# One 256 KB write per copy pair of the sent experts, first-half reads ahead of the second's, two more banks for the last products

## The chip, the cores and the metric

The kernel runs on one core of a Trainium2 chip, in one launch. The metric is the device time in microseconds (us). The host only lays arrays out, and that is not timed. TensorE (PE) multiplies and transposes, VectorE (DVE), ScalarE (ACT) and GpSimd (POOL) work on elements, and SyncE (SP) issues nearly all DMAs. All data is float32 at the interface.

## The reference

A gated block on 16 batches of 128 tokens with 256 channels: x gains tanh(g) times a causal cross attention (16 heads), and then tanh(g) times a mixture of experts on the layer norm of the result. The expert part decides this case:

```python
grouped = x.reshape(B, g, t, d)                     # 64 groups of t = 32 tokens
logits = jnp.einsum('bgtd,des->bgtes', grouped, controller) + tie
perm = (logits == jnp.max(logits, axis=-3, keepdims=True))   # one token for each expert e and set s
dispatched = jnp.einsum('bgtd,bgtes->bgesd', grouped, perm)
inner = relu(jnp.einsum('bgesd,desf->bgesf', dispatched, f1) + bias)     # 32 experts, 4 sets, 32 wide
intermediate = jnp.einsum('bgesf,esfd->bgesd', inner, f2)
out = jnp.einsum('bgesd,bgtes->bgtd', intermediate, perm)
```

Every group of 32 tokens has 128 slots (32 experts x 4 sets), and each slot picks one token. There are 64 groups, so the experts' results are 64 x 128 rows of 256 floats, 8 MB.

## The kernel before

The attention runs up to about 160 us. The routing (logits, choice, gathering the chosen tokens into `routed`) runs to about 200 us, and there SP also loads the weights of the 32 experts into `wx`, 256.5 KB each. What follows is the part that the change touches.

**Expert stage.** The experts are taken in 16 pairs p. For pair p+1 PE computes the inner products (`expert_in`, L856), ACT and DVE apply bias and relu (`hidden`, L1133 and L1441), and for pair p PE computes the outputs (`expert_out`, L874 or L883) into two PSUM banks, of which ACT copies one and DVE the other (`keep_y`, L1143 or L1146, and L1451 or L1454). In the last step a product sums over the 128 slots of one group, so it needs the slots on partitions. The two kinds of pairs come to that in different ways:

- **Kept pairs** (8 of them, real experts 16 to 31) give a transposed output that is copied back into `routed`. At the end PE transposes it (`transpose_y`, L915, 16 blocks) and ACT (three blocks of four) or DVE (every fourth) copies it to partitions 0 to 63 of `y0` or `yw` (L1161, L1468).
- **Sent pairs** (`SENT`, real experts 0 to 15) go through DRAM. Both copies of a pair, one for each t, hold on 128 partitions (c, g) = 2 x 64 the rows of two experts. `send_rows` (L401) writes each copy as two DMAs of 64 partitions and 128 KB, so a pair has four DMAs. `y_rows` is a DRAM tensor [64 slots][64 groups][256 floats]. `load_rows` (L412) reads it back with slots on partitions 64 to 127, in 4 quarters (two sent pairs each) by 2 halves of the groups: `late` = 0 fills `y0` (blocks 0 to 7), `late` = 1 fills `yw`, which lies over expert weights and so also waits for the first 8 pairs. Each of the 8 reads has 512 KB.

There are YR = 4 buffers for sent copies. SP executes its program in order: a wait in it holds back all that follows. Its order is sends 0, 1, 2, load (0, early), sends 3, 4, load (1, early), sends 5, 6, load (2, early), send 7, load (0, late), load (3, early), loads (1 to 3, late), and then the 16 stores of the result (L433).

**Last stage.** PE runs transposes 0 to 3 and then, for each block b, transpose b+4 and `combine(b)` (L930): eight small matmuls of the one-hot `permT` with `y0` or `yw`. Combine 0 waits for the four early loads, combine 8 for the four late ones. Its result goes to bank b % 2. DVE adds it times the gate to `xs` (L1477), SP stores it. Transposes use banks 2 to 7 in turn. With two banks, combine b waits until DVE has done b - 2:

```python
if b >= 2:
    pe.wait_ge(yo_ready, b - 1)
```

The order of slots inside `routed` and `permT` follows from how POOL rearranges the routing weights (L556, four small copies) and from `EXPERTS`, the order in which experts are placed.

Of the kernel before, what the change touches and what calls it, by code (L numbers as in the profile page):

```python
# [21 lines left out]
ALU = mybir.AluOpType  # L22
# [4 lines left out]
NB = 16  # L27
E = 256
# [9 lines left out]
T = 32  # L38
# [18 lines left out]
PAIRS = NE // 2  # L57
HALF = P // 2
BIAS_SETS = 4
SENT = (0, 1, 3, 4, 6, 7, 9, 10)  # L60
KEPT = tuple(p for p in range(PAIRS) if p not in SENT)
EXPERTS = tuple(e for p in range(PAIRS) for e in
                ((SENT.index(p) // 2 + 4 * (SENT.index(p) % 2), SENT.index(p) // 2 + 4 * (SENT.index(p) % 2) + 8) if p in SENT
                 else (PAIRS + 2 * KEPT.index(p), PAIRS + 2 * KEPT.index(p) + 1)))
YR = 4
OVER = 4 * KH * E * 2 + (1 + 2 * 3) * KH * P - 4 * P
G2 = GROUPS // 2
# [8 lines left out]
def build(nc, x, ctxT, wattn, gbo, ctrl, wexp, constf, out):  # L76
    with ExitStack() as ctx, ExitStack() as early, ExitStack() as routing:
# [23 lines left out]
        tg = sb("tg", [P, 2])  # L101
# [71 lines left out]
        def columns(e, c):  # L173
            return bank[e % HR][:, 0:2 * GROUPS].rearrange("p (k c x) -> p c k x", c=2, k=2)[:, c]

        y_rows = nc.dram_tensor("y_rows", (HALF, GROUPS, E), F32).ap()
        sent = [[ring[:, i, t, :] for t in range(2)] for i in range(2)] + [[xn[:, 2 * t:2 * t + 2, :].rearrange("p a x -> p (a x)") for t in range(2)],
                [u[:, :, :, :].rearrange("p a h x -> p (a h x)") for u in (rp, ctrl2)]]

# [103 lines left out]
        def _(sp):  # L283
# [106 lines left out]
            def send_rows(q):  # L390

                p = SENT[q]
                first = EXPERTS[2 * p]
                for t in range(2):
                    if t == 0:
                        sp.wait_ge(y_kept_act, p + 1)
                    else:
                        sp.wait_ge(y_kept_dve, p + 1)
                    for c in range(2):
                        at = (2 * c + t) * 16 + first  # L400
                        sp.dma_start(y_rows[at:at + 9:8].rearrange("e g j -> g e j"),  # L401
                                     sent[q % YR][t][c * HALF:(c + 1) * HALF].rearrange("g (e j) -> g e j", e=2))\
                            .then_inc(y_sent[q % YR], 16)

            def load_rows(quarter, late):

                for q in (2 * quarter, 2 * quarter + 1):
                    sp.wait_ge(y_sent[q % YR], 4 * 16 * (q // YR + 1))
                if late:

                    sp.wait_ge(e_done, PAIRS // 2)
                sp.dma_start((y0, yw)[late][HALF + quarter::4, :].rearrange("s (k x) -> s k x", k=2),  # L412
                             y_rows[quarter::4].rearrange("s (k l x) j -> s k l (x j)", k=2, l=2)[:, :, late])\
                    .then_inc(y_loaded[late], 16)

            send_rows(0)
            send_rows(1)
            send_rows(2)
            load_rows(0, 0)
            send_rows(3)  # L420
            send_rows(4)
            load_rows(1, 0)
            send_rows(5)
            send_rows(6)
            load_rows(2, 0)
            send_rows(7)
            load_rows(0, 1)
            load_rows(3, 0)
            for quarter in range(1, 4):
                load_rows(quarter, 1)  # L430
            for b in range(NB):
                sp.wait_ge(yo_ready, b + 1)
# [5 lines left out]
        def _(pool):  # L438
# [90 lines left out]
            for n in range(SLOTS_N):  # L529
                s, g = n % 8, n // 8  # L530
                if n == 3 or s % 4 == 0 and 1 <= n // 4 - 1 < NB:
                    split_max(n // 4 - 1 if n > 3 else 0)
                if 0 <= n - LT < CH:
                    drop_above(n - LT)
                if s % 4 == 0 and 0 <= n // 4 - 4 < NB:
                    split_out(n // 4 - 4)
                if n == 3 or s == 1 and 2 <= g + 1 < NG2:
                    low_part(qp, 2, qr, 1, g + 1, qm_ready, ql_ready)
                if s == 3 and g + 2 < NG2:
                    low_part(kp, 0, kr, 1, g + 2, km_ready, kl_ready)  # L540
                if n == 16:
                    weight_low(WO)
                if s % 4 == 2 and n // 4 < NB:
                    if n == 2:
                        pool.wait_ge(bo_ready, 1)
                    bias_x(n // 4)
                if n == CH - 8:
                    pool.wait_ge(consts_loaded, 16)
                    pool.tensor_tensor(parity[:, :], groupmask[:, 0:2], groupmask[:, 2:4], ALU.add).then_inc(parity_step, 1)
                    pool.wait_ge(parity_step, 1)  # L550
                    pool.tensor_scalar(shut[:, :], parity[:, :], -1.0, -SHUT, ALU.add, ALU.mult).then_inc(parity_step, 1)
                    pool.wait_ge(small_loaded, 16)
                    for k in range(2):
                        for c in range(2):
                            at = (1 - k) * HALF + c * 32
                            last = pool.tensor_copy(  # L556
                                ctrl_sb[:, :, at:at + 32].rearrange("p h (t e) -> p h t e", t=2),
                                ctrl_in[:, :, k * HALF:(k + 1) * HALF].rearrange("p h (e t c) -> p c h t e", t=2, c=2)[:, c])
                    last.then_inc(ctrl_ready, 1)
                if s == 5 and g + 3 < NG2:  # L560
                    context_low(g + 3)
                if CH <= n < CH + 3:
                    split_rows(n - CH, n - CH)
# [22 lines left out]
        def _(pe):  # L586
# [254 lines left out]
                route(b)  # L841


            def expert_in(e):

                kind, at = int(EXPERTS[e] < PAIRS), EXPERTS[e] % PAIRS
                pe.wait_ge(wx_loaded[e], 16)
                if e >= HR:

                    if e % 2 == 0:  # L850
                        pe.wait_ge(h_ready_act, (e - HR) // 2 + 1)
                    else:
                        pe.wait_ge(h_ready_dve, (e - HR) // 2 + 1)
                for h in range(KH):
                    for t in range(2):
                        last = pe.matmul(bank[e % HR][t * HALF:(t + 1) * HALF, 0:2 * GROUPS],  # L856
                                         wx[:, e, h * P + t * HALF:h * P + (t + 1) * HALF],
                                         routed[:, h, kind].rearrange("p k s x -> p (k s) x")[:, at + 16 * t::32, :],
                                         start=(h == 0), stop=(h == KH - 1),
                                         tile_position=(0, t * HALF), skip_group_check=True)  # L860
                last.then_inc(h_done, 1)
# [36 lines left out]
                expert_out(p)  # L898


            BC = bank[0:2]

            def kept(b):

# [14 lines left out]
            def combine(b):  # L919
                late = b // (NB // 2)  # L920
                kept(b)
                if b % (NB // 2) == 0:

                    pe.wait_ge(y_loaded[late], 4 * 16)
                if b >= 2:
                    pe.wait_ge(yo_ready, b - 1)
                for g in range(NG):
                    k, i = g // 2, g % 2
                    at = k * YK + (b % (NB // 2) * 2 + i) * E
                    last = pe.matmul(BC[b % 2][g * T:(g + 1) * T, 0:E],  # L930
                                     permT[:, b, g * T:(g + 1) * T],
                                     (y0, yw)[late][:, at:at + E], start=True, stop=True, tile_position=(0, g * T))
                last.then_inc(c_done, 1)
# [12 lines left out]
        def _(act):  # L946
# [189 lines left out]
            def keep_y(p):  # L1136
                act.wait_ge(e_done, p + 1)
                if p in SENT:
                    q = SENT.index(p)
                    if q >= YR:  # L1140

                        act.wait_ge(y_sent[q % YR], 4 * 16 * (q // YR))
                    act.activation(sent[q % YR][0], bank[4 + 2 * (p % 2)], ACT.Copy).then_inc(y_kept_act, 1)  # L1143
                else:
                    at = KEPT.index(p) * 2 * G2
                    act.activation(by_set[:, 0, :, :, at:at + 2 * G2],  # L1146
                                   bank[4 + 2 * (p % 2)].rearrange("p (h c x) -> p h c x", h=KH, c=4), ACT.Copy)\
                        .then_inc(y_kept_act, 1)
# [18 lines left out]
        def _(dve):  # L1167
# [276 lines left out]
            def keep_y(p):  # L1444
                dve.wait_ge(e_done, p + 1)
                if p in SENT:
                    q = SENT.index(p)
                    if q >= YR:

                        dve.wait_ge(y_sent[q % YR], 4 * 16 * (q // YR))  # L1450
                    dve.tensor_copy(sent[q % YR][1], bank[5 + 2 * (p % 2)]).then_inc(y_kept_dve, 1)  # L1451
                else:
                    at = KEPT.index(p) * 2 * G2
# [19 lines left out]
            for b in range(NB):  # L1473
                if b % 4 == 1 and b + 4 < NB:
                    keep_ys(b + 4)
                dve.wait_ge(c_done, b + 1)
                dve.scalar_tensor_tensor(xs[:, b, :], bank[b % 2][:, 0:E], tg[:, 1:2], xs[:, b, :], ALU.mult, ALU.add)\  # L1477
                    .then_inc(yo_ready, 1)


# [51 lines left out]
```

## Time and profile before

| | |
|---|---|
| median of 3 runs | 263.15 us (263.0 to 264.95) |
| the profiled execution | 263.96 us |
| its span, first to last instruction | 262.2 us |
| mean granted TensorE clock | 0.979 of full speed |
| PE busy | 219.7 us, 84% |
| DVE busy | 202.1 us, 77% |
| ACT busy | 166.3 us, 63% |
| POOL busy | 128.9 us, 49% |

Times in the trace count from the start of the span; 1.76 us of the profiled execution lie outside it. A busy share is a mean over stages that have different limits. So what counts is, in each stage, which wait ends last. DMA-issuing instructions are not counted as busy, but they take time on SP, and the trace shows each one with its start and duration. "Landing" of a DMA counts from the start of its issue.

### The profile page before, as it was taken

The page shows a single profiled execution, that of the slowest core. Times are in us where ns is not written, and L with a number is a line of the kernel's source. Part 1 is how long each engine was busy: PE and PEld are TensorE (multiplying, and loading weights), DVE is VectorE, ACT ScalarE, POOL GpSimd, SP SyncE. Part 2 cuts the span into 40 slices and gives each one's busy share as a digit, 9 for nine tenths or more (in the row PEclk, how much of TensorE's full clock was granted, in tenths as well). Part 3 has the DMA queues.
Part 4 walks back from the last instruction along what each step waited for, and adds up shares of the span by engine and source line. Part 5 has one row for each costly group of instructions (what it writes and reads, how often), then busy time and mean ns, then how long its engine had stood idle before and what let it go on. Part 6 is the DMA issues. An engine that isn't in the chain of part 4 may idle for free.

```text
span 262.2 us, 7559 instructions
## 1 busy us (share of the span) xinstructions
PE 219.7 (84%) x2849; PEld 171.3 (65%) x2850; DVE 202.1 (77%) x472; ACT 166.3 (63%) x356; POOL 128.9 (49%) x243
## 2 busy tenths in 40 slices
PE   0474687798987999999899999969998999985992
PEld 0464576576765788787677777747776777872550
DVE  4896847789999699696899899999995555553563
ACT  2633766768667868596678775338786555546570
POOL 5652165658746767886487969446572000000000
PEclk9997979999999999999999999999999999998899
DMA  7747689931434344325220000018994587999723
GB/s 213 213 100 201 166 222 227 232 108 50 135 106 135 85 134 110 90 61 143 65 61 6 6 4 6 2 35 314 388 384 168 120 187 211 245 241 202 186 99 124
DMA packets 32231, 37.92 MB, mean 145 GB/s; under 512 B 4099, under 2 KB 27331, under 8 KB 31939
## 3 DMA queue, kind: packets, MB, share of 16 engines
q1 hardware_dynamic: 31661, 36.82, 50.9%
q10 hardware_dynamic: 534, 0.61, 0.8%
q8 instruction: 23, 0.38, 0.7%
q14 instruction: 13, 0.11, 0.1%
HBM read 18.26 MB, written 6.29 MB: 94 GB/s over the span
## 4 chain that ended last, share of the span: by engine, by line
PE 30%; DVE 19%; POOL 17%; issue 12%; DMA 11%; ACT 7%; SPq 3%; ACTq 0%; POOLq 0%; DVEq 0%
POOL pT L481 6%; DVE rsum L1275 4%; PE banks L731 4%; PE banks L753 4%; PE banks L930 3%; DMA y_rows<-ctrl 3%; PE banks L915 3%; PE banks L856 3%; DVE nmax L1267 3%; PE banks L602 3%; DMA y<-y_rows 2%; SPq L401 2%; DMA xs<-in_x_dram 2%; PE banks L711 2%; ACT pT L1022 2%
## 5 line engine op out<-in xcount | busy, mean ns | idle before, releaser
L481 POOL TENSOR_SCALAR_AFFINE_SELECT pT<-pT 128x512 f32<-128x512 f32 x64 | 40.8, 640 | 34.6 <-ACT pT L1022 34.3
L1267 DVE TENSOR_REDUCE nmax<-banks 128x4 f32<-128x512 f32 x64 | 43.7, 682 | 14.8 <-PE banks L665 14.7
L1027 ACT ACTIVATE banks<-cb 128x512 f32<-128x512 bf16 x62 | 37.0, 597 | 12.8 <-DVE nmax L1267 11.1
L1022 ACT ACTIVATE pT<-banks 128x512 f32<-128x512 f32 x64 | 37.5, 586 | 3.0 <-PE banks L682 2.9
L711 PE MATMUL banks<-pT,va 128*32 128x128 f32 x512 | 27.3, 285 | 0.9 <-POOL pT L481 0.8
L1275 DVE RECIPROCAL rsum<-banks 128x256 f32<-128x256 f32 x16 | 27.9, 1746 | 0.0
L665 PE MATMUL banks<-kst,qst 96*128 96x128 bf16 x256 | 25.4, 222 | 2.1 <-ACT banks L1027 2.1
L682 PE MATMUL banks<-qst,kst 99*128 99x128 bf16 x256 | 25.4, 221 | 1.2 <-DMA qst<-nT 1.0
L711 PE MATMUL banks<-pT,ones 128*32 128x128 f32 x512 | 25.7, 273 | 0.0
L1115 ACT ACTIVATE routed<-banks 128x512 f32<-128x512 f32 x30 | 17.2, 626 | 5.6 <-PE banks L753 5.6
L594 PE MATMUL banks<-cf,xn 128*128 128x128 f32 x32 | 6.0, 317 | 17.2 <-DVE xn L1220 14.2
L1042 ACT ACTIVATE onh<-on 128x256 fp32r<-128x256 f32 x16 | 6.7, 417 | 20.1 <-DVE on L1281 19.9
L665 PEld LDWEIGHTS banks<-kst,qst 96*128 96x128 bf16 x256 | 17.0, 99 | 3.5 <-ACT banks L1027 2.9
L682 PEld LDWEIGHTS banks<-qst,kst 99*128 99x128 bf16 x256 | 15.2, 98 | 5.3 <-issue 1.3
L856 PE MATMUL banks<-routed,wx 128*64 128x128 f32 x256 | 17.3, 278 | 0.8 <-ACT routed L1115 0.8
L1220 DVE TENSOR_SCALAR xn<-xs,mv,rs 128x256 f32<-128x256 f32 x32 | 16.8, 531 | 0.1
L856 PEld LDWEIGHTS banks<-routed,wx 128*64 128x64 f32 x256 | 13.7, 136 | 4.4 <-issue 2.7
L594 PEld LDWEIGHTS banks<-cf,xn 128*128 128x128 f32 x32 | 4.1, 159 | 17.9 <-issue 9.0
L711 PEld LDWEIGHTS banks<-pT,ones 128*32 128x32 f32 x512 | 15.3, 110 | 0.0
L711 PEld LDWEIGHTS banks<-pT,va 128*32 128x32 f32 x512 | 10.1, 108 | 7.9 <-POOL pT L481 1.3
L1477 DVE SCALAR_TENSOR_TENSOR xs<-banks,tg,xs 128x256 f32<-128x256 f32 x16 | 7.5, 483 | 9.4 <-PE banks L930 9.3
L505 POOL TENSOR_TENSOR onl<-on,onh 128x256 fp32r<-128x256 f32 x16 | 11.7, 732 | 2.9 <-ACT onh L1042 2.9
(133 smaller groups left out, 624.4 us busy)
## 6 DMA issues: line engine op xcount, KB each, us to landing
wx<-in_wexp_dram SPq DMA_DIRECT2D x32, 256.5 KB, 8.1
kst<-kp SPq DMA_DIRECT2D x48, 128.0 KB, 2.6
qst<-qp SPq DMA_DIRECT2D x48, 128.0 KB, 2.4
cT<-in_ctxT_dram SPq DMA_DIRECT2D x8, 256.0 KB, 3.3
y_rows<-ring SPq DMA_DIRECT2D x16, 128.0 KB, 3.4
y<-y_rows SPq DMA_DIRECT2D x4, 512.0 KB, 5.3
wx<-y_rows SPq DMA_DIRECT2D x4, 512.0 KB, 8.8
out_dram<-xs SPq DMA_DIRECT2D x16, 128.0 KB, 1.9
```

The costliest lines, as they stand in the source:

```text
L481: pool.affine_select(p, p, [[0, HC], [1, P]], ALU.is_ge, 0.0, base=0, channel_multiplier=-1)\
L505: pool.tensor_tensor(onl[:, b % 2], on[:, b % 2], onh[:, b % 2].bitcast(F32), ALU.subtract)\
L665: last = pe.matmul(to[:, j * P:(j + 1) * P], qst[0:SROWS, g % STACKS, h, b % 2, :], kst[0:SROWS, g % STACKS, h, b % 2, :], start=False, st ...
L682: last = pe.matmul(to[:, j * P:(j + 1) * P], kst[0:TROWS, g % STACKS, h, b % 2, :], qst[0:TROWS, g % STACKS, h, b % 2, :], start=True, sto ...
L711: last = pe.matmul(BO[b % 2][j * DP:(j + 1) * DP, at + o * P:at + (o + 1) * P], left, pT[:, n % PR, j * P:(j + 1) * P], start=(e == 0 and ...
L856: last = pe.matmul(bank[e % HR][t * HALF:(t + 1) * HALF, 0:2 * GROUPS], wx[:, e, h * P + t * HALF:h * P + (t + 1) * HALF], routed[:, h, ki ...
L1022: act.activation(pT[:, n % PR, :], BT[n % 2], ACT.Exp, scale=float(D) ** -0.5).then_inc(p_ready, 1)
L1027: act.activation(BS[n % 2], causal, ACT.Copy).then_inc(mask_placed, 1)
L1115: last = act.activation(by_group(t, b), by_column(bank[((3, 6), (4, 5))[b % 2][t]]), ACT.Copy)
L1220: dve.tensor_scalar(xn[:, b % 4, :], xs[:, b, :], mv[:, b, 0:1], rs[:, b:b + 1], ALU.subtract, ALU.mult).then_inc(ready, 1)
L1267: dve.tensor_reduce(nmax[:, b % 2, :].rearrange("p (e j o) -> p e o j", e=2, o=KH)[:, e, o], BS[n % 2].rearrange("p (j t) -> p j t", j=HC) ...
L1275: dve.reciprocal(rsum[:, :, :], BO[b % 2][:, E:2 * E].rearrange("p (h t) -> p h t", h=KH))\
```

## The change

- `SENT` becomes pairs 0, 1, 2, 4, 5, 6, 8, 9, where it was 0, 1, 3, 4, 6, 7, 9, 10. The number of sent pairs stays 8.
- The slots are laid out in another order, so that a whole copy (128 partitions, two experts) is one DMA of 256 KB. Sent pair q fills rows 8q to 8q + 7 of `y_rows`, and a quarter is 16 rows that lie together.
- SP's order becomes sends 0 to 4, early load 0, send 5, early load 1, send 6, early load 2, send 7, early load 3, and then late loads 0 to 3.
- The routing weights are rearranged by three POOL copies, one of 64 columns per half and two of 32.
- `expert_in` reads the sent experts' columns of `routed` through a pattern with one more level.
- Combines 12 and 13 go to banks 6 and 7, which the transposes no longer need by then. Combines 12 and 13 wait for no earlier DVE result, 14 and 15 for the one four blocks (10, 11) back.

```diff
-SENT = (0, 1, 3, 4, 6, 7, 9, 10)
+SENT = (0, 1, 2, 4, 5, 6, 8, 9)
+        by_copy_rows = y_rows.rearrange("(i t c) g j -> t (c g) i j", t=2, c=2)
...
-                    for c in range(2):
-                        at = (2 * c + t) * 16 + first
-                        sp.dma_start(y_rows[at:at + 9:8].rearrange("e g j -> g e j"),
-                                     sent[q % YR][t][c * HALF:(c + 1) * HALF].rearrange("g (e j) -> g e j", e=2))\
-                            .then_inc(y_sent[q % YR], 16)
+                    sp.dma_start(by_copy_rows[t, :, first:first + 2, :],
+                                 sent[q % YR][t].rearrange("p (e j) -> p e j", e=2)).then_inc(y_sent[q % YR], 16)
...
-                             y_rows[quarter::4].rearrange("s (k l x) j -> s k l (x j)", k=2, l=2)[:, :, late])\
+                             y_rows[rows].rearrange("s (k l x) j -> s k l (x j)", k=2, l=2)[:, :, late])\
...
-            send_rows(0)
-            send_rows(1)
-            send_rows(2)
+            for q in range(5):
+                send_rows(q)
             load_rows(0, 0)
-            send_rows(3)
-            send_rows(4)
+            send_rows(5)
             load_rows(1, 0)
-            send_rows(5)
             send_rows(6)
             load_rows(2, 0)
             send_rows(7)
-            load_rows(0, 1)
             load_rows(3, 0)
-            for quarter in range(1, 4):
+            for quarter in range(4):
                 load_rows(quarter, 1)
...
-                    for k in range(2):
-                        for c in range(2):
-                            at = (1 - k) * HALF + c * 32
-                            last = pool.tensor_copy(
-                                ctrl_sb[:, :, at:at + 32].rearrange("p h (t e) -> p h t e", t=2),
-                                ctrl_in[:, :, k * HALF:(k + 1) * HALF].rearrange("p h (e t c) -> p c h t e", t=2, c=2)[:, c])
+                    pool.tensor_copy(ctrl_sb[:, :, HALF:].rearrange("p h (j q) -> p h q j", q=4),
+                                     ctrl_in[:, :, 0:HALF].rearrange("p h (q j) -> p h q j", q=4))
+                    for c in range(2):
+                        last = pool.tensor_copy(
+                            ctrl_sb[:, :, c * 32:(c + 1) * 32].rearrange("p h (t e) -> p h t e", t=2),
+                            ctrl_in[:, :, HALF:].rearrange("p h (e t c) -> p c h t e", t=2, c=2)[:, c])
...
+            def sent_at(e, t):
+                return ((e % 4) * 4 + 2 * t) * 4 + e // 4
...
-                                         routed[:, h, kind].rearrange("p k s x -> p (k s) x")[:, at + 16 * t::32, :],
+                                         routed[:, h, 1, :, sent_at(at, t):sent_at(at, t) + 5:4, :] if kind else
+                                         routed[:, h, 0].rearrange("p k s x -> p (k s) x")[:, at + 16 * t::32, :],
...
-            BC = bank[0:2]
+            BC = [bank[b % 2 if not 12 <= b < 14 else b - 6] for b in range(NB)]
...
-                if b >= 2:
+                if 2 <= b < 12:
                     pe.wait_ge(yo_ready, b - 1)
+                elif b >= 14:
+                    pe.wait_ge(yo_ready, b - 3)
```

## Rows read from the trace of the kernel before

**Rows 1.** Waits from 200 to 262.2 us: who waited for whom, total us, times, longest.
```profile
PE banks L930 <- DMA y<-y_rows: 3.0, 1, 3.0
PE banks L930 <- DVE xs L1477: 0.5, 2, 0.3
```

**Rows 2.** Chain that ended last, from 228 us: start us, us, what.
```profile
231.22 2.65 DMA y_rows<-ctrl
...
233.94 5.96 DMA y<-y_rows
...
240.04 0.64 PE banks L930 x8
...
245.20 0.57 PE banks L930 x8
...
254.90 0.61 PE banks L930 x8
```

**Rows 3.** Windows: us, busy us (count) of PE, PEld, DVE, ACT, POOL, clock, DMA share, GB/s.
```profile
200.00:234.00 34.00, 33.36 (x448) 26.88 (x448) 18.47 (x49) 17.62 (x49) 0.68 (x2) 1.00 0.71 180
237.00:240.00 3.00, 0.00 (x0) 0.00 (x0) 0.07 (x1) 2.92 (x6) 0.00 (x0) 1.00 1.06 213
241.00:244.00 3.00, 3.00 (x23) 1.25 (x22) 2.08 (x4) 0.40 (x1) 0.00 (x0) 0.50 0.96 197
245.00:254.00 9.00, 9.00 (x94) 4.92 (x93) 5.75 (x12) 6.20 (x11) 0.00 (x0) 1.00 0.43 136
...
218.50:219.00 0.50, 0.50 (x12) 0.33 (x8) 0.22 (x1) 0.50 (x3) 0.00 (x0) 1.00 1.18 395
```

**Rows 4.** Timeline of the expert stage: start us, us, engine, line, operation [idle before].
```profile
203.35 0.69 DVE L1451 COPY ring<-banks 128x512 f32<-128x512 f32 x1 [0.60 <-PE banks L874]
205.44 0.69 DVE L1451 COPY ring<-banks 128x512 f32<-128x512 f32 x1 [0.59 <-PE banks L874]
...
222.23 0.69 DVE L1451 COPY xn<-banks 128x512 f32<-128x512 f32 x1 [0.59 <-PE banks L874]
```

**Rows 5.** Timeline of SP: issue of each write (L401) and load (L412).
```profile
207.33 0.61 SPq L401 DMA_DIRECT2D y_rows<-ring  x1
207.98 1.90 SPq L401 DMA_DIRECT2D y_rows<-ring  x1
...
228.67 1.52 SPq L401 DMA_DIRECT2D y_rows<-rp  x1
```

**Rows 6.** Landings by source line: L401, the 32 writes; then L412, the 8 loads.
```profile
DMA to landing us min/median/max: 2.4/3.0/5.2
...
DMA to landing us min/median/max: 4.9/5.7/11.1
```

**Rows 7.** The same views of L287 (input loads) and L433 (stores): issue ns, min/median/max.
```profile
L287 SPq DMA_DIRECT2D xs<-in_x_dram x5: 442/471/707, 0.8 to 42.9; - x5
...
L433 SPq DMA_DIRECT2D out_dram<-xs x16: 332/333/417, 241.2 to 258.7; - x16
```

**Rows 8.** Timeline of the last stage's start.
```profile
234.51 2.49 PE L915 MATMUL banks<-cf,routed 128*128 128x128 f32 x20 [0.88 <-DVE routed L1454]
235.23 4.86 ACT L1161 ACTIVATE y<-banks 64x512 f32<-64x512 f32 x8 [0.96 <-PE banks L915]
235.68 1.39 DVE L1468 COPY y<-banks 64x512 f32<-64x512 f32 x2 [1.32 <-PE banks L915]
```

**Rows 9.** Timeline of the end.
```profile
255.54 0.92 DVE L1477 SCALAR_TENSOR_TENSOR xs<-banks,tg,xs 128x256 f32<-128x256 f32 x2 [0.73 <-PE banks L930]
...
258.20 0.48 DVE L1477 SCALAR_TENSOR_TENSOR xs<-banks,tg,xs 128x256 f32<-128x256 f32 x1 [0.41 <-PE banks L930]
```

**Rows 10.** Groups of POOL by form; L468 copies 128x128 with two inputs.
```profile
L468 POOL TENSOR_TENSOR wl<-w,wh 128x128 fp32r<-128x128 f32 x4 | 2.0, 536 | 3.2 <-ACT wh L970 3.2
L556 POOL COPY ctrl<-ctrl 128x64 f32<-128x64 f32 x4 | 1.0, 290 | 0.1
```

**Rows 11.** Groups by form from 200 us: PE reading `routed`.
```profile
L856 PE MATMUL banks<-routed,wx 128*64 128x128 f32 x256 | 17.3, 278 | 0.8 <-ACT routed L1115 0.8
```

More of the change, by code:

```diff
@@ L59 @@
 BIAS_SETS = 4
-SENT = (0, 1, 3, 4, 6, 7, 9, 10)
+SENT = (0, 1, 2, 4, 5, 6, 8, 9)
 KEPT = tuple(p for p in range(PAIRS) if p not in SENT)
-EXPERTS = tuple(e for p in range(PAIRS) for e in
-                ((SENT.index(p) // 2 + 4 * (SENT.index(p) % 2), SENT.index(p) // 2 + 4 * (SENT.index(p) % 2) + 8) if p in SENT
-                 else (PAIRS + 2 * KEPT.index(p), PAIRS + 2 * KEPT.index(p) + 1)))
+EXPERTS = tuple(2 * SENT.index(p) + i if p in SENT else PAIRS + 2 * KEPT.index(p) + i
+                for p in range(PAIRS) for i in range(2))
 YR = 4
@@ L398, in send_rows @@
                         sp.wait_ge(y_kept_dve, p + 1)
-                    for c in range(2):
-                        at = (2 * c + t) * 16 + first
-                        sp.dma_start(y_rows[at:at + 9:8].rearrange("e g j -> g e j"),
-                                     sent[q % YR][t][c * HALF:(c + 1) * HALF].rearrange("g (e j) -> g e j", e=2))\
-                            .then_inc(y_sent[q % YR], 16)
+                    sp.dma_start(by_copy_rows[t, :, first:first + 2, :],
+                                 sent[q % YR][t].rearrange("p (e j) -> p e j", e=2)).then_inc(y_sent[q % YR], 16)
             def load_rows(quarter, late):
                 for q in (2 * quarter, 2 * quarter + 1):
-                    sp.wait_ge(y_sent[q % YR], 4 * 16 * (q // YR + 1))
+                    sp.wait_ge(y_sent[q % YR], 2 * 16 * (q // YR + 1))
                 if late:
                     sp.wait_ge(e_done, PAIRS // 2)
+                rows = slice(quarter * 16, (quarter + 1) * 16)
                 sp.dma_start((y0, yw)[late][HALF + quarter::4, :].rearrange("s (k x) -> s k x", k=2),
-                             y_rows[quarter::4].rearrange("s (k l x) j -> s k l (x j)", k=2, l=2)[:, :, late])\
+                             y_rows[rows].rearrange("s (k l x) j -> s k l (x j)", k=2, l=2)[:, :, late])\
                     .then_inc(y_loaded[late], 16)
-            send_rows(0)
-            send_rows(1)
-            send_rows(2)
+            for q in range(5):
+                send_rows(q)
             load_rows(0, 0)
-            send_rows(3)
-            send_rows(4)
+            send_rows(5)
             load_rows(1, 0)
-            send_rows(5)
             send_rows(6)
@@ L929, in combine @@
                     at = k * YK + (b % (NB // 2) * 2 + i) * E
-                    last = pe.matmul(BC[b % 2][g * T:(g + 1) * T, 0:E],
+                    last = pe.matmul(BC[b][g * T:(g + 1) * T, 0:E],
                                      permT[:, b, g * T:(g + 1) * T],
@@ L1140, in keep_y @@
                     if q >= YR:
-                        act.wait_ge(y_sent[q % YR], 4 * 16 * (q // YR))
+                        act.wait_ge(y_sent[q % YR], 2 * 16 * (q // YR))
                     act.activation(sent[q % YR][0], bank[4 + 2 * (p % 2)], ACT.Copy).then_inc(y_kept_act, 1)
@@ L1448, in keep_y @@
                     if q >= YR:
-                        dve.wait_ge(y_sent[q % YR], 4 * 16 * (q // YR))
+                        dve.wait_ge(y_sent[q % YR], 2 * 16 * (q // YR))
                     dve.tensor_copy(sent[q % YR][1], bank[5 + 2 * (p % 2)]).then_inc(y_kept_dve, 1)
@@ L1476, in _ @@
                 dve.wait_ge(c_done, b + 1)
-                dve.scalar_tensor_tensor(xs[:, b, :], bank[b % 2][:, 0:E], tg[:, 1:2], xs[:, b, :], ALU.mult, ALU.add)\
+                dve.scalar_tensor_tensor(xs[:, b, :], bank[b % 2 if not 12 <= b < 14 else b - 6][:, 0:E], tg[:, 1:2], xs[:, b, :], ALU.mult, ALU.add)\
                     .then_inc(yo_ready, 1)
```

## The prediction, made before the changed kernel ran

> **What bounds the kernel now.** I read the waits of the last 60 us first, then the chain of waits, then SP's own timeline. The waits show one stall of PE that is large: combine 0 waits 3.0 us for a load from `y_rows` [rows 1]. The chain says which load that is, and when: the last write of a sent pair is issued at 231.22, lands, releases early load 3 at 233.94, and 5.96 us later that load is there and combine 0 runs at 240.04 [rows 2]. Two things make it late. The pair that it needs is the eleventh of sixteen, and SP falls behind. The copies of a sent pair come every 2.09 us where two such pairs follow one another (203.35, 205.44 in rows 4), but a pair has four writes that begin 0.65 us apart, 2.6 us, and now and then an issue takes 1.5 to 1.9 us instead of 0.61 [rows 5]. The copy of the last sent pair, pair 10, ends at about 225.0 (pair 9's ends at 222.92 [rows 4], plus a period of 2.09), and yet its last write is issued only at 231.22: SP is 6.2 us behind.
>
> The stall costs more than itself. With PE idle for 3.0 us the granted clock, which was 1.00 from 200 to 234, is 0.50 of 2.4 GHz (the lower level, 1.2 GHz) from 241 to 244 and back at 1.00 from 245 on [rows 3]. Three periods of transpose and combine take 245.20 - 240.04 = 5.16 us, where the eight that follow take (254.90 - 245.20) / 8 = 1.21 us each [rows 2].
>
> Behind that, PE sets the pace at 1.21 us a block to combine 11 (254.90), and in the tail the two banks do: combines wait for DVE [rows 1], and DVE's last five results come at 255.54 and up to 258.20 in pairs with gaps [rows 9].
>
> **The change part by part, on the profiled execution (span 262.2, time 263.96).**
>
> *Writes.* 32 DMAs of 128 KB become 16 of 256 KB with the same pieces of 1 KB, twice as many in each. The trace has no such issue. Lower bound: 0.33 us, a store of 128 rows [rows 7]; upper bound: twice the present write, 1.22 us [rows 5]. The input loads, of 256 or 512 rows of 1 KB, take 0.44 to 0.71 us [rows 7], so the count of rows hardly matters; the shape of the pattern seems to. The pattern stays, so I take 0.65 us with its gap. A pair then costs SP 1.3 us, less than PE's period of 2.09 us, and SP waits for copies rather than the other way round.
>
> *Pairs and order.* The last sent pair is pair 9, whose DVE copy ended at 222.92 in this trace [rows 4]. Nothing ahead of it changes in length, since kept and sent pairs cost PE the same. SP's program after: early load 2 is just ahead of send 7 and waits for the writes of sends 4 and 5. Pair 6's copies end at 222.92 - 3 x 2.09 = 216.6, its second write is issued by 217.3 and lands after 2.4 to 5.2 us [rows 6], by 222.5 at the latest. Load 2 then goes out at about 222.5, and send 7 at 222.9 and 223.6. That write lands after 2.4 to 5.2 us, so early load 3 is issued at 226.0 to 228.8. It lands after 4.9 to 5.96 us [rows 2, 6] (the 11.1 us in that row is of a late load, queued behind others): between 230.9 and 234.8.
>
> *Where PE is by then.* Transposes 0 to 4 end at 234.51 + 2.49 = 237.00 [rows 8], and that end does not depend on the loads. ACT's copy of block 0 ends at 235.23 + 4.86 / 4 = 236.45, and DVE's of block 1 at 237.07 [rows 8], ahead of the combines that need them. So combine 0 starts at 237.0, not 240.04: **3.04 us**. The margin over the load's latest landing is 2.2 us, and 6 us over its earliest. ACT needs 1.21 us for a block and has three of four, 0.91 us a block; DVE has 1.39 / 4 + 0.48 = 0.83. Both stay under PE's 1.21.
>
> *The clock.* With no idle stretch the first three periods should run at 1.21 us as the later ones do: 5.16 - 3 x 1.21 = **1.53 us**. Bounds: nothing, if the clock falls all the same, and 1.53. I take the whole, since the rows show 1.00 through 34 us of dense work before the stall [rows 3]. Combine 11 then starts at 237.0 + 11 x 1.21 = 250.3, 4.6 us before its 254.90.
>
> *Late loads.* Late load 0 no longer stands ahead of early load 3. All four go out between about 229 and 234. At the rate of the window in which only such loads ran, 213 GB/s from 237 to 240 [rows 3], 2 MB take 9.8 us, so they are there by some 245 us; combine 8 runs at 237.0 + 8 x 1.21 = 246.7. Hidden, though not by much: were they as late as before relative to their issue, PE would wait 1 us or so there.
>
> *Banks 6 and 7.* Before, DVE starts block 11 at 255.54 and block 15 at 258.20. A pair of DVE results takes 0.92 and one 0.48, so 0.44 us apart [rows 9]. Combines 12 to 15 now need DVE's results of 10 and 11 at the most, and PE needs 0.57 us for one at the most [rows 2]; in the pairs it already keeps up with DVE's 0.44. DVE would start block 15 at 255.54 + 4 x 0.44 = 257.30: **0.90 us**. Bounds: 0.4, if PE gives one per 0.57 us, and 0.9. The store behind it takes what it took.
>
> *POOL.* Four copies take 1.0 us together. One of 128x128 (no more than the 0.54 us of the two-input L468) and two of 128x64 (0.25 each) give 0.8 to 1.04 us [rows 10]: within 0.2 us either way, and I take nothing. *The columns of `routed`:* L856 already reads four runs of 32 floats at a stride; a further level changes no count of columns. I take nothing. The three slot orders cost no instruction.
>
> Sum: 3.04 + 1.53 + 0.90 = 5.5 us, so the profiled execution would take 263.96 - 5.5 = 258.5. The median of the runs is 0.8 under the profiled one, 263.15, and so the forecast is **257.7 us**. What is uncertain there: if the runs near 263.0 did not have the whole clock loss, the median gains less.
>
> A rule that speaks against the first step: the Trainium skill, "DMA: Bandwidth & Descriptors", section "Issuing engines are not separate DMA queues", says that the time a sequencer takes to start a DMA is usually small beside the transfer. The trace disagrees here: issues of 0.65 us for 128 KB make 200 GB/s, while loads and writes together reached 395 GB/s in a window [rows 3]. By the rule the writes would be bound by the DMA engines and the change would give only what the order and `SENT` give, which is the second rival below.
>
> **Rivals.**
>
> 1. *The clock falls all the same, or the runs never had the whole loss.* For it: 0.8 us between median and profiled run. Against: the clock falls only after the stall [rows 3]. Gain 3.04 + 0.90 = 3.9: 259.2 us. Chance 0.12.
> 2. *Issue or transfer stays the bound.* If a 256 KB issue costs 1.22 us, a pair costs SP 2.5 us as before; with two of the slow issues (+1.3 us each [rows 5]) SP ends send 7 at about 228.7, the write lands by 232, load 3 by 238.0. Combine 0 then starts at 238.0, the stall is 1 us, and the gain 2.0 + 0.9 + the clock's 0 to 1.5: 260.2 to 258.7 us. If instead the DMA engines move 1 KB pieces no faster than 200 to 230 GB/s, 4 MB of writes and three early loads end near 231, load 3 by 237: nearly nothing lost. Chance 0.10.
> 3. *The load is no earlier.* Something that the trace doesn't show (the writes' landing growing with their size, SP waiting at early load 2) holds load 3 until about 240. Only the tail is gained: 262.2 us. It takes a delay of over 5 us on the bounds above. Chance 0.05.
> 4. *Slower.* PE reads the four runs of a sent expert's columns with one more level and loses time on each of L856's 128 sent matmuls. At present one costs 17.3 / 256 = 0.068 us of PE's time [rows 11]. It decides from 5.5 / 128 = 0.043 us each; at twice that it would cost 8.7 us, net +3.2: 266.4 us. For it: no row has this pattern. Against: the same four runs at a stride cost nothing visible now [rows 11]. Chance 0.04.
>
> The forecast itself, 256.5 to 258.9 us, has 0.69.
>
> **How the numbers follow.** About 1% (2.6 us) is what a measurement of this kernel can tell from no change. The forecast, rival 1 and most of rival 2 are faster by over 1%: 0.69 + 0.12 + 0.07 = 0.88. The rest of rival 2 and rival 3 are within 1%: 0.08. Slower: 0.04. The range 256.5 to 260.3 takes in the forecast, rival 1 and most of rival 2, and leaves out misses of the sum by more than 1.2 us downward.
>
> **What would show it.** After: 16 write issues of about 0.61 us, SP waiting for copies; early load 3 issued at 226 to 229 and landed by 235; no wait of L930 on a DMA; 20 transposes at 234.5 and combine 0 right behind at 237; a granted clock of 1.00 from 237 to 246; a period of 1.21 us from the first block; the last five DVE results 0.44 us apart; L856 with an unchanged mean of 278 ns. The prediction is wrong if combine 0 or combine 8 still waits for a load, if the clock falls in that stretch, or if the expert stage's end moves from 234.4.

## The result

The changed kernel takes 260.04 us (median of 4 runs, 258.35 to 261.0), the kernel before beside it 264.05 us (263.0 to 266.31). The ratio is 0.9865, 95% interval 0.9818 to 0.9912. Two more measurements of the same two kernels (`after_again` and `after_third` below, on two chips) gave 0.9838 (0.9808 to 0.9868) and 0.9812 (0.976 to 0.9865). A ratio compares only runs within 1.5% of the fastest run of the same kernel, while a median is one of all runs. So the change is worth 1.6%, about 4.2 us, and the forecast was 2.1%, 5.5 us. The forecast time, 257.7, was 2.3 us too low: 0.9 of it because the kernel before takes 264 us and more in larger samples, not 263.15, and 1.5 because the gain was smaller.

The chain of waits of the changed kernel, from the first transpose of the last stage on (start us, us, what):

```profile
236.92 2.49 PE banks L914 x20
239.41 0.57 PE banks L931 x8
...
243.05 0.57 PE banks L931 x8
...
252.76 0.61 PE banks L931 x8
253.37 0.03 issue
253.39 2.21 DVE xs L1478 x5
```

It holds no DMA any more. Combine 0 follows the transposes at once (2.49 us after their start; before it was 5.53 [rows 2, 8]), three periods take 243.05 - 239.41 = 3.64 us (before 5.16), and DVE's last five results are one run of 2.21 us. The windows show that the granted clock stays at 1.00, the level of 2.4 GHz (columns as in rows 3):

```profile
240.00:241.00 1.00, 1.00 (x12) 0.59 (x12) 0.82 (x2) 0.96 (x3) 0.00 (x0) 1.00 0.81 164
243.00:244.00 1.00, 1.00 (x13) 0.59 (x12) 0.32 (x1) 0.96 (x3) 0.00 (x0) 1.00 1.30 262
```

SP's timeline (L399 writes, L410 loads) and, below it, its waits in that stretch:

```profile
216.86 0.36 SPq L399 DMA_DIRECT2D y_rows<-ring  x1
217.26 0.47 SPq L399 DMA_DIRECT2D y_rows<-ring  x1
...
225.15 0.52 SPq L410 DMA_DIRECT2D y<-y_rows  x1
225.71 1.69 SPq L399 DMA_DIRECT2D y_rows<-rp  x1
227.44 0.48 SPq L399 DMA_DIRECT2D y_rows<-ctrl  x1
232.12 0.52 SPq L410 DMA_DIRECT2D y<-y_rows  x1
232.75 0.53 SPq L410 DMA_DIRECT2D wx<-y_rows  x1
```

```profile
SPq L405 <- DMA y_rows<-ctrl: 4.1, 1, 4.1
SPq L405 <- DMA y_rows<-ring: 1.1, 1, 1.1
```

A 256 KB write is issued in 0.36 us and a second behind it in 0.47, less than a 128 KB one took before (0.61 [rows 5]). SP now waits for the copies. Early load 3 is issued 4.8 us ahead of the first transpose (before: 0.6) and lands 5.5 us later, 1.8 us before combine 0.

And yet the profiled execution is only 4.0 us shorter in its span, 258.2 against 262.2, although the stretch from the first transpose to the end went from 27.7 to 21.3 us. Of these 6.4 us, 3.04 are the stall, 1.52 the clock, 0.94 the banks, and 0.9 lie behind DVE's last result, where the last store took 3.5 us to the end of the span before and takes 2.6 now; no part of the change touches that store. On the other side, the first transpose itself comes 2.4 us later, at 236.92 instead of 234.51. The page's row of the granted clock, 40 slices of the span, shows where; first before, then after:

```profile
PEclk9997979999999999999999999999999999998899
```

```profile
PEclk9997779599999999999999999999999999999999
```

Before has its late fall (8 8, behind the stall), after has none; but in slices 5 to 8, 26 to 52 us, where both kernels run the same instructions, after has 7 7 9 5 where before has 9 7 9 9. The first row-sum reciprocal of DVE starts at 54.43 us before and at 56.98 after.

### The profile page after: what moved, and what is told of

It is laid out like the page before. It is cut to its first block, busy times and chain, and to the rows that moved or that the text cites. A ratio compares the mean times of both kernels' runs of the same rounds, so it can differ in the third digit from the quotient of the medians.

```text
span 258.2 us, 7540 instructions
## 1 busy us (share of the span) xinstructions
PE 221.8 (86%) x2849; PEld 174.9 (68%) x2850; DVE 204.4 (79%) x472; ACT 166.5 (64%) x356; POOL 128.9 (50%) x242
## 4 chain that ended last, share of the span: by engine, by line
PE 41%; DVE 20%; POOL 15%; issue 11%; ACT 6%; DMA 4%; ACTq 0%; SPq 0%; POOLq 0%; DVEq 0%
PE banks L854 6%; POOL pT L475 6%; DVE rsum L1276 4%; PE banks L914 4%; PE banks L725 4%; PE banks L747 4%; PE banks L596 3%; PE banks L882 3%; PE banks L873 3%; PE banks L705 3%; DVE nmax L1268 3%; PE banks L931 3%; DMA w<-in_wattn_dram 2%; PE banks L618 2%; DMA xs<-in_x_dram 2%
## 5 line engine op out<-in xcount | busy, mean ns | idle before, releaser
L659 PE MATMUL banks<-kst,qst 96*128 96x128 bf16 x256 | 26.1, 226 | 3.0 <-ACT banks L1028 2.8
L705 PE MATMUL banks<-pT,va 128*32 128x128 f32 x512 | 27.7, 289 | 0.7 <-POOL pT L475 0.7
L676 PE MATMUL banks<-qst,kst 99*128 99x128 bf16 x256 | 25.8, 224 | 0.3 <-ACT pT L1023 0.3
L659 PEld LDWEIGHTS banks<-kst,qst 96*128 96x128 bf16 x256 | 17.6, 101 | 4.4 <-ACT banks L1028 3.6
L596 PE MATMUL banks<-xTh,wh 128*128 128x256 f32 x32 | 11.8, 368 | 2.5 <-DVE xTl L1260 2.5
```

The source lines that it names most:

```text
L596: last = pe.matmul(to[:, o * E:(o + 1) * E], stationary, moving, start=(q == 0), stop=(q == len(parts) - 1))
L659: last = pe.matmul(to[:, j * P:(j + 1) * P], qst[0:SROWS, g % STACKS, h, b % 2, :], kst[0:SROWS, g % STACKS, h, b % 2, :], start=False, st ...
L676: last = pe.matmul(to[:, j * P:(j + 1) * P], kst[0:TROWS, g % STACKS, h, b % 2, :], qst[0:TROWS, g % STACKS, h, b % 2, :], start=True, sto ...
L705: last = pe.matmul(BO[b % 2][j * DP:(j + 1) * DP, at + o * P:at + (o + 1) * P], left, pT[:, n % PR, j * P:(j + 1) * P], start=(e == 0 and ...
```

## The experiments

All stages below are read from one profiled execution of each kernel, in us. "T0" is the start of the first transpose of the last stage. `before_look1` and `before_look2` are two more profiled executions of the kernel before.

| kernel | T0 | T0 to combine 0 | combine 0 to 3 | T0 to end |
|---|---|---|---|---|
| before | 234.5 | 5.53 | 5.16 | 27.7 |
| before_look1 | 235.7 | 5.32 | 3.70 | 24.6 |
| before_look2 | 237.6 | 4.71 | 5.08 | 25.9 |
| banks_only | 236.0 | 5.39 | 5.05 | 26.1 |
| filler | 236.8 | 6.61 | 3.70 | 25.9 |
| order_only | 237.8 | 3.71 | 3.79 | 24.7 |
| writes_only | 236.3 | 3.20 | 3.71 | 23.5 |
| old_pairs | 234.8 | 5.04 | 3.70 | 24.1 |
| late_load | 236.7 | 4.83 | 5.11 | 25.3 |
| by_expert | 236.0 | 2.48 | 3.63 | 21.2 |
| after | 236.9 | 2.49 | 3.64 | 21.3 |
| after_again | 237.9 | 2.48 | 3.64 | 21.7 |
| after_third | 238.9 | 2.49 | 3.64 | 21.6 |

**Is the later start the change's doing?** The changed and the unchanged kernel were run again.

> The changed kernel once more, timed in more rounds. Theory A: the stretch from the first transpose of the last stage to the end is fixed by the change (21.3 us, where before has 27.7) and what differs beside it lies in the first 54 us, where the code is the same and the granted clock falls by chance: then the mean gain over many rounds is 5 to 6.5 us, ratio 0.976 to 0.981, and another profile of the same kernel has another start (the first row-sum reciprocal anywhere from 53 to 58 us). Theory B: the changed kernel itself loses 2.5 us in its first part (another placement of code or data): then that reciprocal is at 57 us again and the ratio stays near 0.985.

> The kernel before once more, one look. Theory A (the profiled execution of before was an unusual one: early start of the last stage, full clock loss behind the stall): the first transpose comes later than 234.5 us, near the 236 to 238 us of five other profiled executions whose code is the same up to 145 us, and the stretch from there to the end is 26 to 27.7 us. Theory B (the changed kernel is slower in its first 54 us): the first transpose comes at 234.5 us again.

> The same kernel, a second look, to see how the stall (T0 to combine 0, 5.5 us), the three periods behind it (5.2 us with the clock at half, 3.6 without) and the last store (3.5 us or 2.6) vary. Theory A: the stall is the same within 0.3 us, the periods behind it are 5.0 to 5.2 in most looks. Rival 1 of the prediction: in some looks the clock stays at 1.00 and they take 3.7.

> The changed kernel beside the two above on the same chip: from the first transpose to combine 0 2.5 us, to the end 21.2 to 21.8 us, and the first row-sum reciprocal anywhere from 54.4 to 58 us. Runs near 260.2 us.

The ratio of after_again is 0.9838, outside the 0.976 to 0.981 of theory A and with an interval down to 0.9808; its row-sum reciprocal starts at 57.98 us. Both are nearer to what theory B expected. The three profiled executions of the kernel before have that reciprocal at 54.4 to 55.3 us and T0 at 234.5, 235.7 and 237.6, the three of the changed one have 57.0 to 58.0 and 236.9, 237.9 and 238.9. With the other kernels, whose first 145 us are the same code too, the difference shrinks: the six with the old slot layout average 55.4 us for the reciprocal and 236.4 for T0, the seven with the new one 56.5 and 236.8. The profiled execution on which the prediction was built has the earliest T0 of all thirteen. So these executions leave theory B open; the warmed kernels below decide it. From T0 on, the changed kernel repeats within 0.5 us and the kernel before varies by 3.1 us, in the stall (4.7 to 5.5), behind it, and in the landing of the last store. In before_look2 the clock fell again (1.01 and 1.05 us where 0.57 and 0.64 are the times at full clock):

```profile
242.28 0.64 PE banks L930 x8
242.91 0.64 PE banks L915 x4
243.56 1.01 PE banks L930 x8
244.57 1.05 PE banks L915 x4
```

In before_look1 it did not, with a stall of 2.8 us:

```profile
241.01 0.64 PE banks L930 x8
241.65 0.64 PE banks L915 x4
242.29 0.57 PE banks L930 x8
242.86 0.64 PE banks L915 x4
```

**One part at a time.** `order_only` is before with two edits, the new `SENT` and the new order of SP; `writes_only` is after with both old and two banks; `banks_only` is before with the edits of `BC` and its waits.

```diff
-SENT = (0, 1, 3, 4, 6, 7, 9, 10)
+SENT = (0, 1, 2, 4, 5, 6, 8, 9)
```

> The kernel before with only the new choice of sent pairs and the new order of SP; writes stay 128 KB (four a pair, 2.6 us of SP), banks stay two. Theory A (both SP's backlog and the late pair held the load back): pair 9's last write is issued at about 229 instead of 231.2 of the kernel before, early load 3 at 231.5 instead of 233.9, so combine 0 starts 2 to 3 us after where the kernel before has it relative to the transposes: stall 0.5 to 1.5 us, the clock's loss partly gone; gain 2 to 4 us from the first transpose on. Theory C (the order alone was enough): no stall, gain 4.6 us. Theory D (only the number of writes mattered): gain under 1 us.

> The changed kernel with the old choice of pairs, the old order of SP and two banks, so only the 256 KB writes with their slot layout. Pair 10's copy ends 9.4 us before the first transpose (225.1 of 234.5 in the kernel before). Theory A: writes are issued at once, land within 5 us, early load 3 is issued about 3.5 to 4 us before the first transpose and lands 1.5 to 2.5 us after it, before combine 0 is due at +2.5: no stall or under 0.5 us, the clock stays at 1.00, gain 4.6 us from the first transpose on. Theory C (order decides): late load 0, which stands ahead of early load 3, holds it back and a stall of over 1 us stays.

> The kernel before with banks 6 and 7 for combines 12 and 13. Theory A: the last five DVE results come 0.44 us apart, 0.9 us less from combine 11 on, the stall of 3.0 us and the clock at 0.50 behind it stay as they were. In the runs a gain of 0.3%, about what three rounds can't tell. Rival: the store queue or its landing takes it back, and the stretch from combine 11 to the end stays at 7.3 us.

Ratios: order_only 0.9898 (0.9858 to 0.9938), writes_only 0.987 (0.9826 to 0.9915), banks_only 0.9925 (0.9867 to 0.9983). Against the mean stall of 2.7 us in three executions of the kernel before, `order_only` has 1.2 and `writes_only` 0.7. With order and pairs alone SP issues its last write at 231.67, still late because pairs cost it 2.6 us, and combine 0 waits 1.2 us:

```profile
231.67 4.11 DMA y_rows<-ctrl
...
235.85 5.50 DMA y<-y_rows
241.35 0.14 issue
```

With the writes alone early load 3 goes out at 233.78 and lands 5.6 us later, and combine 0 runs 0.13 us behind that, 0.7 us after it could have:

```profile
233.78 0.52 SPq L410 DMA_DIRECT2D y<-y_rows  x1
239.50 0.64 PE L933 MATMUL banks<-y,permT 128*32 128x256 f32 x8 [0.71 <-ACT y L1164]
```

The profile puts these 0.71 us down to ACT, which copied until 239.45; but the copy that combine 0 needs is ACT's first, done by 237.6. Theory A had the load 1 to 1.5 us earlier and the stall under 0.5, theory C had over 1. The parts overlap: order and pairs alone take 1.5 of the mean 2.7 us, the writes alone 2.0, the rest needs both. banks_only shows DVE's five results in 2.21 us and the stall and the clock's fall as before; the tail is 0.94 us shorter, as expected (0.3%). By its ratio it gains 0.75%, with an interval that reaches to 0.2%; by the medians of all runs, 263.82 and 264.35 us, it gains 0.2%.

**The choice of pairs.** The changed kernel with only the old `SENT`:

> The changed kernel with the old choice of sent pairs (the last is pair 10, not 9), and with the new order, the 256 KB writes and the new banks. Theory A: the last send and early load 3 come one pair's time (2.1 us) later than in the changed kernel; early load 3 lands at about +2.5 to +3.2 us after the first transpose, so the choice of pairs is worth a stall of 0 to 0.7 us. Rival E (in the run with the writes alone it was late load 0, ahead in the queue, that held early load 3): no stall here, combine 0 at +2.5.

Both expectations fell. Combine 0 waits 2.5 us. The chain (start us, us, what) says why:

```profile
227.39 6.77 DMA y_rows<-ctrl
...
234.22 5.52 DMA y<-y_rows
```

The last write is issued 7.4 us ahead of T0 (9.5 in the changed kernel), as its pair comes 2.1 us later, and it lands after 6.8 us and not 4.6. Early load 2 stands right ahead of it (in the timeline of SP, old_pairs):

```profile
226.19 0.52 SPq L410 DMA_DIRECT2D y<-y_rows  x1
226.76 0.58 SPq L399 DMA_DIRECT2D y_rows<-rp  x1
227.39 0.47 SPq L399 DMA_DIRECT2D y_rows<-ctrl  x1
```

All 18 traces of this case say the same about that load. The last write lands 6.4 to 8.0 us after the issue of early load 2, whether it is issued 1.2 us behind it (and lands after 5.4 to 6.8 us) or 3.8 us behind it (2.7 to 2.9 us), and always after that load has landed. So the time of early load 3 follows from that of early load 2, and this one goes out 11.8 us ahead of T0 in the changed kernel, 8.7 in old_pairs and 7.1 in before. In the changed kernel and in old_pairs it waits for the second write of send 5, which belongs to pair 6 with the new `SENT` and to pair 7 with the old one. That the load's 512 KB hold the write is the reading of these traces; no run moved load 2 alone.

In this one profiled execution of old_pairs the choice of pairs is worth 2.5 us of stall, once the order is the new one. The order by itself is not shown to gain anything: old_pairs has writes_only's pairs and writes and the new order, and stalls for 2.5 us where writes_only stalls for 0.7. No run has the new pairs in the old order.

**Cut in two again.** The changed kernel with each copy in two DMAs by expert:

```diff
+                    for i in range(2):
+                        sp.dma_start(by_copy_rows[t, :, first + i, :],
+                                     sent[q % YR][t][:, i * E:(i + 1) * E]).then_inc(y_sent[q % YR], 16)
```

> The changed kernel with each 256 KB write cut in two again, by expert instead of by partition: 32 writes of 128 KB, each 128 partitions times 1 KB, the shape of the stores. Theory A (SP's time per pair and the place of the last sent pair decide, not the number of writes): an issue takes 0.33 us and 0.42 with its gap, a pair 1.7 us, under the 2.09 us period, so there is no stall and the kernel equals the changed one within 0.5 us. Rival (many small writes clog the transfers): early load 3 lands later and combine 0 waits.

From T0 on it is the changed kernel (2.48, 3.63, 21.2 us), with 32 writes as before. Its issues take 0.32 to 0.49 us, 128 rows of 1 KB over 128 partitions; the kernel before needed 0.61 for 128 rows of 1 KB over 64 partitions. So neither the number of writes nor that of rows mattered. The shape shortened both the issue and the landing of an undisturbed write (1.7 to 1.9 us, against 2.4 before), and this run does not part the two. Its ratio, 0.9898 with an interval of 0.9779 to 1.0018, says nothing beside that.

**The stall put back.** The changed kernel with `sp.wait_ge(e_done, PAIRS)` ahead of early load 3:

> The changed kernel with one wait more: SP issues early load 3 only after the last expert product, about 0.9 us before the first transpose, as the kernel before did by its backlog. All else of the change stays. Theory A: combine 0 starts 4.7 to 5.2 us after the first transpose instead of 2.5; the clock falls behind the stall or not, so the stretch from the first transpose to the end grows from 21.3 us by 2.2 to 2.7 us without the clock's fall and by up to 4.2 us with it; the runs lose 0.9 to 1.6% against the changed kernel. Rival: something else of the change (slot layout, columns of the experts) made the gain, and the stretch stays within 1 us of 21.3.

The ratio to the kernel before is 0.9952 (0.9923 to 0.9981), against 0.981 to 0.984 of the changed kernel: 1.1 to 1.4% come from this one load. The chain has it, with the clock's fall behind it:

```profile
235.84 5.54 DMA y<-y_rows
241.39 0.14 issue
241.52 0.64 PE banks L932 x8
242.16 0.64 PE banks L915 x4
242.81 0.89 PE banks L932 x8
243.69 1.05 PE banks L915 x4
244.74 1.01 PE banks L932 x8
```

**The clock behind the stall.** The kernel before with work for PE in the stall, output unused:

```diff
+                if b == 0:
+                    for _ in range(22):
+                        pe.transpose(bank[1][:, 0:P], ident, ident)
                 combine(b)
```

> The kernel before with 22 transposes of the identity into bank 1 between transposes 0 to 4 and combine 0. They fill 2.75 us of the 3.0 us in which PE waits for the load; their output is used by nothing. Theory A: combine 0 starts no earlier (5.5 us after the first transpose), the granted clock stays at 1.00, the next three periods take 3.64 instead of 5.16 us, and the runs gain up to 1.5 us (0.6%). Rival 1 of the prediction (the runs mostly don't have that loss): the profile shows the same, but the runs gain under 0.5 us.

The stall is there (6.6 us from T0, the load took 6.6 us in this execution), the three periods take 3.70 us. The ratio, 0.9969 (0.9912 to 1.0025), could not tell the rival.

**The start made steady.** PE waits at 18 to 24 us for the second pair of normalized blocks, 5.1 us in before, and comes out of it at the lower level: the granted clock is 0.50 from 23 to 25.8 us. Twenty transposes of the identity into bank 0 went there:

```diff
+            for _ in range(20):
+                pe.transpose(bank[0][:, 0:P], ident, ident)
             transpose_x(1, bank[3])
```

> The changed kernel with 20 transposes of the identity into bank 0, whose output is used by nothing, while PE waits for the second pair of normalized blocks at 18 to 24 us. Theory A (the different start of the runs comes from where the granted clock falls in the first 56 us): the clock stays at 1.00 from 20 to 28 us, where nine profiled executions had 0.59 to 0.79, the matmuls of that stretch end 1 to 1.5 us earlier after the wait, and the runs gain up to 1.5 us, unless the later falls (32 to 56 us) take it back. Rival F (the start is set by the loads and by DVE, the clock is only a sign): the first row-sum reciprocal stays between 54.4 and 58 us and the runs stay within 0.3%.

> The changed kernel with the 20 transposes ahead of the wait at 18 to 24 us, once more, beside the three above: near 257.9 us and 0.9755 of the kernel before.

Ratios 0.9755 (0.9723 to 0.9786) and 0.9788 (0.9731 to 0.9845), medians 257.93 and 258.73 us: about 2 us faster than the changed kernel, somewhat more than the up to 1.5 us of theory A. The granted clock is 1.00 from 20 to 28 us in warm. In the timeline of the kernel before and of warm, PE comes out of the wait like this (start us, us, what [idle before]):

```profile
22.99 1.12 PE L594 MATMUL banks<-cf,xn 128*128 128x128 f32 x4 [5.12 <-DVE xn L1220]
23.75 0.56 PE L602 MATMUL banks<-cTh,wh 128*128 128x256 f32 x1
```

```profile
20.12 2.35 PE L764 MATMUL banks<-cf 128*128 128x128 f32 x20
23.92 0.66 PE L588 MATMUL banks<-cf,xn 128*128 128x128 f32 x4 [1.46 <-DVE xn L1223]
24.33 0.37 PE L596 MATMUL banks<-cTh,wh 128*128 128x256 f32 x1
```

The same on the kernel before, without and with the filler in the stall, and once more with 20 transposes ahead of PE's first wait:

> The kernel before with the same 20 transposes of the identity, output unused, ahead of the wait at 18 to 24 us. Theory A (the start varies by chance and equally in both kernels): the first row-sum reciprocal comes at 54 to 55 us, the runs gain about 2 us (0.8%) on the kernel before, as the changed kernel did (0.9755 against 0.983), and stand 4.5 us above warm_again. Theory B (the changed kernel had lost something in its start that the filling gave back): no gain here, and warm_again is over 6 us faster.

> The same kernel and also 22 unused transposes into bank 1 in the stall ahead of combine 0. Theory A (the clock's fall behind the stall is in about two runs of three): 1.0 us (0.4%) faster in the runs than warm_before, the three periods behind the stall 3.7 us in the profile. Rival 1 of the prediction (the runs mostly don't have it): under 0.4 us. The full term of the prediction would be 1.5 us.

> The changed kernel with the 20 transposes of warm_again and 20 more as soon as the identity is loaded, at 4 to 9 us, when PE waits for the first normalized blocks; outputs unused. If PE's 256-column matmuls of 11 to 19 us take 0.41 us because the clock is low there, they take 0.28 us now and the start gains 1 to 2.5 us (0.4 to 1%) where PE sets the pace; if loads and DVE set it, under 0.5 us.

warm_before has 0.9903 (0.9858 to 0.9948), so the kernel before gains 1% by the same lines, and between it and warm_again lie 1.2% by the ratios, 3 us (4.4 us by the medians of all runs, 263.12 and 258.73), where theory B had over 6. T0 comes at 235.2 and 234.2 us in warm_before and warm_before_filler, and at 234.4 and 235.0 in warm and warm_again. The start of the changed kernel had lost nothing of its own: theory B falls. warm_before_filler has 0.9828 (0.9776 to 0.9881): 0.75% less than warm_before, 2 us, with intervals that overlap. That speaks for a clock term in the runs and against rival 1; filler without the warming gained 0.3%, so its size stays open. warm_both, 0.9756 (0.97 to 0.9813), is no different from warm_again. The transposes at 3.8 to 7.8 us do not bring the clock up for what follows, as this window of warm_both shows (columns as in rows 3, clock 0.50):

```profile
12.00:19.00 7.00, 5.92 (x28) 5.65 (x28) 7.00 (x13) 2.45 (x4) 3.81 (x4) 0.50 0.47 103
```

## Why the prediction was wrong, point by point

- **Direction and place: right.** The load from `y_rows` bound combine 0, and SP's backlog and the late pair made it late. Of the 6.4 us from T0 on in the profiled execution, 5.5 are where the steps put them.
- **The stall, 3.04 us: right in the profiled execution** (5.53 to 2.49 = 3.04), and too large for other executions: two more of the kernel before have 5.32 and 4.71, so it is 2.7 us on the mean of three.
- **The clock, 1.53 us: the step that failed, by its size.** I took the upper bound because the stretch before the stall had run at 1.00, as if every run lost it. Of seven profiled executions with a stall of over 2 us and no filler, five lost it (before, before_look2, banks_only, late_load, and warm_before with 5.16 us) and two did not (before_look1, old_pairs). Over the three executions of the kernel before the three periods take 5.16, 3.70 and 5.08, a mean 1.0 us over 3.64. In the runs the filler gave 0.8 us on the kernel before (0.9969) and about 2 us on the warmed one, each with 1.5 to 2 us of uncertainty, so the runs do not narrow that.
- **The banks, 0.90 us: right.** From combine 11 to the end of DVE's work it was 258.68 - 254.90 = 3.78 us, and is 2.84.
- **The last store, taken to be unchanged: luck in the profiled execution.** Behind DVE's last result the span goes on for 3.5 us before and 2.6 after, and this 0.9 us, in no term of the sum, flattered the measured gain. That part takes 2.1 to 3.7 us in the eight traces of kernels with the old banks and 2.4 to 3.1 in the ten with the new ones, 2.7 us on the mean of either, so it is no gain of the change.
- **POOL, nothing: off by 0.2 us.** In the chain the first copy takes 0.41 us and the other two 0.38, 0.79 against 0.99, and the row-sum reciprocals, 2.59 us later than before until then, are 2.38 us later behind it.
- **An issue, 0.65 us: too high.** It was 0.36 to 0.47. I had bounded it by the 64-partition write; the row of the stores, which I used as the lower bound, was the nearer one. The rule weighed there is that issue time is usually small beside the transfer (the Trainium skill, "DMA: Bandwidth & Descriptors", section "Issuing engines are not separate DMA queues"). At the 395 GB/s of [rows 3], an estimate, 128 KB take 0.33 us, less than the old issue of 0.65 with its gap, and 256 KB take 0.66, more than the new one of 0.36 to 0.47. So the trace speaks against the rule for the old writes and not for the new ones.
- **Early load 3, issued at 226.0 to 228.8: too early.** On before's time axis it was 232.12 - 2.41 = 229.7. Early load 2 went out where I had it (222.7 against 222.5), but I let the last write land 2.4 to 5.2 us after its own issue, and it landed 6.9 us after that load's. One issue of send 7 took 1.69 us, a case that I had put in a rival and not in the sum; it is not the cause, since in warm and writes_only, where send 7 has no such issue, the last write lands 6.8 us after early load 2 too. The margin of 2.2 us to 6 us was 1.8.
- **Late loads hidden: right, narrowly.** The last takes 13.6 us and is there at 248.2; combine 8 runs at 249.1.
- **What failed beyond the terms: the frame.** The sum was made on one execution and moved to a median of three runs by its 0.8 us. That execution had the earliest T0 of thirteen (234.5, mean 236.6) and the longest last stage (27.7 against 24.6 and 25.9). A saving read off it is at the upper end. With the means of three executions the sum is 2.7 + 1.0 + 0.9 = 4.6 us, where it was 5.5; T0 to end went from 26.1 to 21.5 us, 4.6 too, and 0.2 more ahead of T0. The runs say 4.2, and the median of the kernel before moves between 264.05 and 265.12 from one measurement to the next.

What stays open: how large the clock's part is in the runs, why issues of 0.9 to 2.1 us occur now and then, in both kernels, and why the clock falls behind one stall of 2.2 us and not behind one of 2.8.

## What to carry to other kernels

When a queue is behind, count what it spends on each issue against the period of the work that feeds it, and look at what stands directly ahead of the last urgent transfer: the last write here landed after 2.7 us in one kernel and after 6.8 in another, and in all of them 6.4 to 8.0 us after the issue of the 512 KB load ahead of it. Read a saving off more than one execution where the granted clock moves: here one execution overstated it by 30%. Where PE waits for a fixed and known time at the start, some idle-time matmuls were worth as much as half of this change: 2 us for two lines.

## What the hardware showed that I had not expected

- A DMA issue depends more on the shape than on the size: 0.61 us for 128 KB over 64 partitions, 0.36 to 0.47 for 256 KB over 128, 0.32 to 0.49 for 128 KB over 128 (by_expert).
- The record of the granted clock says 1.00 from 11 to 19 us in the changed kernel, while PE's 256-column matmuls take 0.41 us until 18.3 us and 0.28 from 18.7 on. In warm_both, where PE starts at 3.8 us, the same matmuls take 0.41 to 0.42 and the record says 0.50. So a 1.00 ahead of the first change on record is not to be trusted; the durations are.
- Runs of one and the same kernel on one core lie within 261.7 to 265.9 us (23 runs), and the place of the falls of the clock in the first 56 us differs from one execution to the next.
